# Two-layer decoder on one core: load and linear attention in one stage, recurrent weights fetched a stage earlier, four score banks in the second cross attention

## The reference

```python
x = x + linear_attention(layernorm(x))          # 16 heads of 8, causal, feature map elu + 1
x = x + cross_attention_0(layernorm(x), ctx)    # 16 heads of 8, one mask row per sequence
x = x + ternary_ffn(layernorm(x))               # gate and up 512, weights rounded to -1, 0, 1
x = x + mamba(layernorm(x))                     # 4 blocks, inner width 256, 16 states, scan over 256 tokens
x = x + cross_attention_1(ctx, layernorm(x))    # queries 16 heads of 64 from layernorm(x), keys and values from ctx
x = x + moe(layernorm(x))                       # top 2 of 8 experts
```

## Time and profile before

| what | us |
| --- | --- |
| median of 3 runs | 1855.62 |
| the profiled execution | 1858.3 |
| its span, from the first to the last instruction | 1856.6 |
| load stage, to the last VectorE instruction | 40.1 |
| linear attention, 40.3 to | 184.3 |
| cross attention 0, to | 415.6 |
| feed-forward and the norm after it, to | 503.3 |
| mamba, 503.6 to | 1430.7 |
| norm and cross attention 1, to | 1764.8 |
| experts and store, to | 1856.6 |

### The profile page before, as it was taken

How to read it: one execution, slowest core, us unless ns; L and a number is a source line. 1 busy time by engine, 2 the same in 40 slices (tenths; PEclk the granted TensorE clock), 3 DMA queues, 4 the chain that set the end, 5 groups by cost and what they waited for, 6 DMA issues and landing times. The chain is left out here.

```text
span 1856.6 us, 23408 instructions
## 1 busy us (share of the span) xinstructions
PE 1338.0 (72%) x6867; PEld 652.9 (35%) x6867; DVE 1443.7 (78%) x2462; ACT 1106.6 (60%) x2435; POOL 1141.6 (61%) x742
## 2 busy tenths in 40 slices
PE   3788898986655667766666765667655698899878
PEld 2555565653221222211222221222211365566523
DVE  3555588986419999999999999999997577777634
ACT  2444787875636666556666655666644577677630
POOL 2101466650039999999999999999995244444400
PEclk8889899996668778777788877888867899999979
DMA  3000000000044434354334434443431311111000
GB/s 96 1 1 2 1 2 2 1 2 1 21 168 179 153 116 172 140 206 183 125 141 163 177 154 183 180 146 117 168 130 57 130 46 47 64 73 46 1 0 23
DMA packets 68666, 168.04 MB, mean 91 GB/s; under 512 B 20404, under 2 KB 38088, under 8 KB 55112
## 3 DMA queue, kind: packets, MB, share of 16 engines
q1 hardware_dynamic: 65800, 164.34, 24.1%
q10 hardware_dynamic: 2496, 2.36, 0.4%
q0 software_dynamic: 256, 0.01, 0.0%
HBM read 131.03 MB, written 35.65 MB: 90 GB/s over the span
## 5 line engine op out<-in xcount | busy, mean ns | idle before, releaser
L1543 POOL TENSOR_TENSOR ma_hs<-ma_dtuR,ma_Bt 128x1024 f32<-128x1024 f32 x256 | 597.3, 2362 | 30.7 <-PE ps L1619 23.4
L1725 ACT ACTIVATE ps<-ma_dtR,ma_A 128x512 f32<-128x512 f32 x512 | 332.6, 682 | 314.5 <-DVE ma_hs L1867 271.1
L824 POOL TENSOR_TENSOR x_pr<-x_pr,x_rec 128x512 f32<-128x512 f32 x256 | 267.9, 1047 | 288.9 <-DVE x_rec L1064 288.9
L1861 DVE TENSOR_TENSOR_SCAN ps<-ps,ma_hs 128x1024 f32<-128x1024 f32 x176 | 401.8, 2283 | 2.0 <-POOL ma_hs L1543 1.9
L1030 ACT ACTIVATE x_pr<-x_sm,x_mx 128x256 f32<-128x256 f32 x512 | 255.2, 500 | 70.0 <-DVE x_mx L1055 67.3
L1619 PE MATMUL ps<-ma_hs,ma_fold 128*32 128x512 f32 x1024 | 164.4, 772 | 163.5 <-POOL ma_hs L1551 151.1
L1867 DVE TENSOR_TENSOR ma_hs<-ps,ma_Ct 128x1024 f32<-128x1024 f32 x176 | 215.4, 1224 | 6.1
L1586 PE MATMUL ps<-ma_hn,ma_w_tap 128*128 128x512 f32 (+3 forms) x256 | 146.3, 726 | 88.2 <-ACT ma_hn L1749 75.6
L1861 DVE TENSOR_TENSOR_SCAN ma_hs<-ps,ma_hs 128x1024 f32<-128x1024 f32 x80 | 182.5, 2281 | 30.9 <-ACT ps L1725 29.7
L1551 POOL TENSOR_TENSOR ma_hs<-ma_hs,ma_Ct 128x1024 f32<-128x1024 f32 x80 | 188.6, 2358 | 13.6 <-DVE ma_hs L1861 13.6
L886 PE MATMUL ps<-ident,x_pr 128*128 128x128 f32 x1024 | 162.1, 284 | 4.6 <-DVE x_pT L964 4.3
(11 more groups left out here) (303 smaller groups left out, 2231.0 us busy)
## 6 DMA issues: line engine op xcount, KB each, us to landing
ma_dtuR<-ma_dtu_d SPq DMA_DIRECT2D x32, 1024.0 KB, 6.7
ma_dtR<-ma_dt_d SPq DMA_DIRECT2D x32, 1024.0 KB, 8.8
ma_Bt<-ma_bc_d SPq DMA_DIRECT2D x16, 1024.0 KB, 5.1
ma_Ct<-ma_bc_d SPq DMA_DIRECT2D x16, 1024.0 KB, 7.4
ma_dtu_d<-ma_dtu SPq DMA_DIRECT2D x32, 256.0 KB, 2.0
ma_dt_d<-ma_dt SPq DMA_DIRECT2D x32, 256.0 KB, 2.3
keys_d<-ma_kv SPq DMA_DIRECT2D x32, 256.0 KB, 5.0
values_d<-ma_kv SPq DMA_DIRECT2D x32, 256.0 KB, 2.1
```

Of the source, the lines that this page charges most:

```text
L824: pool.tensor_tensor(pr[:, r, :, :], pr[:, r, :, :], rec[:, r, :].unsqueeze(2).broadcast_to([P, 2, L]), ALU.mult).then_inc(pr_done, 1)
L1543: pool.tensor_tensor(hs[:, k % SLOTS, :, :], dtuR[:, unit(f, h), q, :].unsqueeze(1).broadcast_to([P, 2, CH]), rows(Bt, k), ALU.mult).then_ ...
L1725: e = act.activation(c.ps[:, 2 * (k % 2) + a, :], dtR[:, unit(f, h), q, :], ACT.Exp, scale=A[:, (f // QUARTERS) % 2, h, q, no:no + 1])
L1861: dve.tensor_tensor_scan(out, pair(k), slot(k), 0.0, ALU.mult, ALU.add).then_inc(scan_done, 1)
```

## The change

Three edits. First, load and linear attention become one block, `opening_stage`. SP loads x in two halves, then the context, the mask row and the feed-forward weights. TensorE transposes x first; the context is transposed after the first projection. VectorE's work on the mask and the ternary weights is cut into pieces that `for_later(b, m)` puts behind the causal masking of given pairs; TensorE's part of it (`weight_mean`, `ternary_turned`) stands after the first pair of sequence 4 and before the last output projection. Scores j = 0 to 2 also wait for the copies that free their banks. Second, a class `RecurrentWeights` holds the mamba weights for the whole program; for block 0 its transfers are issued and its GpSimd work is done in the feed-forward stage, and `a_exp` is waited for in a part of its own (`rates`). Third, cross attention 1 takes the bank plan of cross attention 0: score pairs alternate between banks 0, 1 and 5, 7, values have bank 4 alone, projections and the output projection share bank 6, and the four projections stand one each at n = 9 to 12.

```diff
-def load_stage(c, g):
...
-def linear_attention_stage(c):
+def opening_stage(c, g):
...
+            @block.sync
+            def _(sp):
+                x = g["x"].rearrange("b (t p) d -> p (b t) d", p=P)
+                sp.dma_start(xt[:, 0:NT // 2, :], x[:, 0:NT // 2, :]).then_inc(x_in0, 16)
+                sp.dma_start(xt[:, NT // 2:NT, :], x[:, NT // 2:NT, :]).then_inc(x_in1, 16)
+                sp.dma_start(ct[:, :, :], g["ctx"].rearrange("b (t p) d -> p (b t) d", p=P)).then_inc(ctx_in, 16)
+                sp.dma_start(mi[:, :, :], g["m0"].rearrange("(a b) k -> a b k", a=1).broadcast_to([P, B, L])
+                             ).then_inc(mask_in, 16)
+                sp.dma_start(wg[:, 0:4, :], g["wg"].rearrange("(t p) d -> p t d", p=P)).then_inc(ffn_in, 16)
+                sp.dma_start(wg[:, 4:8, :], g["wu"].rearrange("(t p) d -> p t d", p=P)).then_inc(ffn_in, 16)
+                sp.dma_start(wd[:, :], g["wd"]).then_inc(ffn_in, 16)
...
+                for h in range(4):
+                    pe.wait_ge(x_in0 if h < 2 else x_in1, 16)
+                    for k in range(4):
+                        mm = pe.transpose(c.ps[:, 4 + h, k * P:(k + 1) * P], xt[:, 4 * h + k, :], c.ident[:, :])
+                    mm.then_inc(x_turned, 1)
+                for h in range(4):
+                    pe.wait_ge((x_dve, x_act)[h % 2], 1 + h // 2)
+                    pe.matmul(c.ps[:, 4 + h, :], c.centre[:, :], c.xT[:, chunk(h)], start=True, stop=True).then_inc(centred, 1)
+                pe.wait_ge(wa_in, 16 * 9)
+                for n in range(2):
+                    for k in range(4):
+                        mm = pe.transpose(c.ps[:, 2 + n, k * P:(k + 1) * P], wa[:, 4 * n + k, :], c.ident[:, :])
+                    mm.then_inc(wa_turned, 1)
+                for h in range(2):
+                    pe.wait_ge(squared, h + 1)
+                    pe.matmul(c.ps[:, h, :], c.average[:, :], sq[:, chunk(h)], start=True, stop=True).then_inc(var_done, 1)
+                pe.wait_ge(wa_copied, 4)
+                pe.wait_ge(squared, 3)
...
+                def context_turned():
+                    pe.wait_ge(ctx_in, 16)
+                    for n in range(4):
+                        for k in range(4):
+                            mm = pe.transpose(c.ps[:, 2 + n, k * P:(k + 1) * P], ct[:, 4 * n + k, :], c.ident[:, :])
+                        mm.then_inc(ctx_turned, 1)
+
+                def weight_mean():
+                    pe.wait_ge(sums, 3)
+                    pe.wait_ge(v_done, 5)
+                    pe.wait_ge(rec_done, 5)
+                    pe.wait_ge(x_done, 3)
+                    pe.matmul(c.ps[:, W, 0:3], c.ones_sq[:, :], part[:, :], start=True, stop=True).then_inc(mean_done, 1)
...
+                def ternary_turned():
+                    pe.wait_ge(ternary, 3)
+                    pe.wait_ge(sc_act, B * NPAIR - 1)
+                    pe.wait_ge(sc_dve, B * NPAIR - 1)
...
                 pe.wait_ge(made, 10)
                 project(0)
+                context_turned()
                 project_values(0)
                 denominator(0)
                 for b in range(B):
                     for m in range(NPAIR):
                         score(b, m)
+                        if b == 4 and m == 0:
+                            weight_mean()
...
                 weigh(B - 1, NG - 1)
+                ternary_turned()
                 out_projection(B - 1)
 
             @block.scalar
             def _(act):
+                for i, n in enumerate(("aq", "ak", "av", "ao", "xq", "xk", "xv", "xo")):
+                    act.dma_start(wa[:, i, :], g[n]).then_inc(wa_in, 16)
+                act.dma_start(wr[:, :], g["rw"]).then_inc(wa_in, 16)
+                act.preload_act_table_set("natural_log_exp_and_others")
...
+                def for_later(b, m):
+                    if (b, m) == (0, 6):
+                        dve.wait_ge(mask_in, 16)
+                        dve.tensor_scalar(c.maskrow[:, :, :], mi[:, :, :], 0.0, MASKED, ALU.is_equal, ALU.mult).then_inc(mask_done, 1)
+                    if (b, m) == (1, 6):
+                        dve.wait_ge(mask_done, 1)
+                        dve.tensor_reduce(c.present[:, :], c.maskrow[:, :, :], AX.X, ALU.max).then_inc(mask_done, 1)
+                    if (b, m) == (2, 0):
...
+                    if (b, m) == (4, 0):
+                        dve.wait_ge(mean_done, 1)
+                        dve.tensor_scalar(c.wmean[:, :], c.ps[:, W, 0:3], 1.0 / (F * P), 1e-5, ALU.mult, ALU.max).then_inc(step, 1)
+                    if (b, m) == (4, 3):
+                        dve.wait_ge(step, 1)
+                        dve.reciprocal(wscale[:, :], c.wmean[:, :]).then_inc(step, 1)
...
+                    if (b, m) == (5, 6):
+                        dve.wait_ge(step, 5)
+                        dve.tensor_scalar(wq[:, :, F:2 * F], wq[:, :, 0:F], ROUND, 1.0, ALU.subtract, ALU.min).then_inc(step, 1)
...
+                        for_later(b, m)
                 divide(B - 1)
+                dve.wait_ge(qturned, 1)
+                dve.tensor_copy(c.wguT[:, :], c.psb(2)[:, 0:8 * P]).then_inc(qcopied, 1)
+                dve.tensor_copy(c.wdT[:, :, :], c.psb(4)[:, 0:4 * P].rearrange("p (t d) -> p t d", t=4)).then_inc(qcopied, 1)
...
-    WO = 6 if small else 7
-    SCORE_BANKS = ((0, 1), (5, 7)) if small else ((0, 1),)
+    WO = 6
+    SCORE_BANKS = ((0, 1), (5, 7))
...
-            a = n - FIRST_UNIT
-            if small:
-                return range(a - 1, a) if 1 <= a <= NP else range(0)
-            return range(min(NP, a * 3 // 2), min(NP, (a + 1) * 3 // 2)) if a >= 0 else range(0)
+            a = n - FIRST_UNIT - 1
...
-            return SCORE_BANKS[(n // 2) % len(SCORE_BANKS)][n % 2]
-
-        def projection_bank(n):
-
-            return 6 if small else 6 + n % 2
+            return SCORE_BANKS[(n // 2) % 2][n % 2]
...
-                    bank = c.ps[:, projection_bank(n), :]
-                    if small and n >= 1:
+                    bank = c.ps[:, WO, :]
+                    if n >= 1 or not first:
                         pe.wait_ge(evac, b * NP + n)
-                    elif n >= 2:
-                        pe.wait_ge(evac, b * NP + n - 1)
-                    elif not first:
-                        pe.wait_ge(evac, b * NP)
-                    if 6 + n == WO and not first and not second:
+                    if n == 0 and not first and not second:
...
-                    if small and (n >= 4 or not first):
-                        pe.wait_ge(max_done, b * NH + n - 2)
-                    elif not small and (n >= 2 or not first):
-                        pe.wait_ge(s_free, b * NH + n)
+                    if n >= 4 or not first:
+                        pe.wait_ge(max_done if small else s_free, b * NH + n - 2)
...
-                    if not small and g % 2 == 0 and (g >= 4 or not first):
-                        pe.wait_ge(oT_done, b * NO + g // 2 - 1)
+                    if not small and g % 2 == 0 and (g >= 2 or not first):
+                        pe.wait_ge(oT_done, b * NO + g // 2)
...
-                                mm = pe.matmul(c.ps[64 * r:64 * r + 64, O0 + h // 4 % 2, at:at + L],
+                                mm = pe.matmul(c.ps[64 * r:64 * r + 64, O0, at:at + L],
...
-                                        c.ps[:, O0 + u % 2, :]).then_inc(oT_done, 1)
+                                        c.ps[:, O0, :]).then_inc(oT_done, 1)
...
+            @block.sync
+            def _(sp):
+                c.weights.load(sp, g, 0)
+
+            @block.gpsimd
+            def _(pool):
+                c.weights.prepare(pool, c, 0)
...
+    def load(self, sp, g, i):
+        b, xb, gq, e32 = i % 2, RANK + 2 * NS, 4, 32
+        done = self.weights_in
+        if i >= 1:
+            sp.wait_ge(self.tap_w, 3 * i)
+            sp.wait_ge(done, self.LOADS * i)
+        sp.dma_start(self.w_in[:, :], g["m_in"][i]).then_inc(done, 16)
+        sp.dma_start(self.cwb[:, :, :], g["m_cw"][i].rearrange("(a c) t -> a c t", a=1).broadcast_to([P, DI, TAPS])).then_inc(done, 16)
...
+    def prepare(self, pool, c, i):
+        b, gq = i % 2, 4
+        pool.wait_ge(self.weights_in, self.LOADS * (i + 1))
+        for h in range(2):
...
-                load(0)
                 kv_weight(sp, 0)
...
-                weights(0)
+                rates(0)
```

397 lines of the change are left out of this document (176 added, 221 removed).

## The result

| | us |
| --- | --- |
| median before, same chip | 1854.9 |
| median after | 1829.99 (1829.32 to 1834.84) |
| ratio after to before | 0.9859, interval 0.984 to 0.9877 |
| the profiled execution after, span | 1829.81, 1828.1 |

A forecast was written before the change was run, and what follows sets the result against it. Small waits set linear attention, with TensorE nearest its limit; VectorE limits mamba. Opening -20.9, recurrent weights -9.5, GpSimd +0.3 and cross attention 1 -3.7 sum to -33.8, from 1855.6 to 1821.8 us, range 1811 to 1834.

The forecast's parts named there:

- First projection: Start of linear attention: with x sent first, the first projection starts at 21.9 in place of 44.84, -22.9 us.
- centre product about 1.05 to its square: Opening's norm: after ScalarE's copy the centre product takes about 1.05 us to its square, reaching 14.0; first average at 15.0.
- Pieces in linear attention: About 10 us of VectorE's mask and ternary weight work moved into linear attention costs +2.0 us, bounds 0 and +10.
- The first rival: Opening's extra VectorE work falls on TensorE's waits, its clock drops, x lands later: +10 us, 1831.8; chance 0.18.
- Recurrent weights: Start of mamba: block 0's weights are ready early, so TensorE begins at 510.6 in place of 520.16, -9.5 us.
- GpSimd beside VectorE: Feed-forward stage: GpSimd's weight work delays a few VectorE SBUF-to-SBUF instructions, +0.3 us, bounds 0 and +2.9.
- Cross attention 1: New plan of score, value and projection banks in cross attention 1: -3.7 us together, bounds -15 and +38.
- Before the first scores: Cross attention 1's first sequence: four projections through one bank take 7.1 us in place of 4.5, +2.4 us.
- The wait of 1.63 goes: Cross attention 1: VectorE's 1.63 us wait at n = 10 goes, since one projection more stood before it.
- The scores of n = 12 come 1.0 - 0.1 earlier: Cross attention 1: one of four projections falls behind the scores of n = 12; over a whole sequence -0.5 us.
- The second rival: Score banks free cross attention 1, TensorE's sum sets it: 2.1 us for each of seven sequences, 1810.6; chance 0.09.
- The third: Cross attention 1: one value bank makes TensorE late at 32 copy waits, +38 us in place of -3.7, 1864; chance 0.04.

The follow-up runs named there:

- e3: Kernel before with only cross attention 1's new plan of banks and projections: 1858.6 us against 1857.27, ratio 1.0008.
- e8: Changed kernel with each long piece of VectorE's mask and weight work in linear attention run twice: 1832.62 us, ratio 0.9870.
- e2: Changed kernel with cross attention 1 back in its old plan of banks and projections: 1830.49 us, ratio 0.9834.
- e5: Changed kernel with GpSimd's weights made at mamba's start and cross attention 1's first four projections in banks 6, 7, 5, 4 without waits: 1823.54 us, ratio 0.9807.
- e6: As e5, with cross attention 1's output projection in four parts and query projections at n = 9, 11, 13, 14: 1814.87 us, ratio 0.9762.
- e10: Changed kernel with GpSimd's weights made at mamba's start and cross attention 1 in its old plan: 1827.97 us, ratio 0.9836.
- e11: As e10, with the output projection in four parts and query projections at n = 9, 11, 13, 14, on the old banks: 1811.5 us, ratio 0.9748.
- e12: As e5, with cross attention 1's four query projections one step later, at n = 10 to 13: 1821.1 us, ratio 0.9803.
- e7: Changed kernel with GpSimd's 2.85 us instruction in the feed-forward stage run twice in a row: ratio 0.9869.
- e1: Opening alone against the kernel before, recurrent weights back in mamba and cross attention 1 in its old plan: 1833.8 us against 1857.27, ratio 0.9859.
- e4: Changed kernel with weight transfers kept in the feed-forward stage but GpSimd's part made at mamba's start: 1833.33 us, ratio 0.9858.
- e9: Changed kernel repeated word for word: 1833.98 us against 1856.64, ratio 0.9872.

## Why the prediction was right or wrong, step by step

The time lay in the range (1811 to 1834), 8 us over the forecast, and faster as forecast. The two gains that made the time, the opening and the recurrent weights, came by their mechanism. But the sum hid errors that ran against each other: cross attention 1 was 11 us off its term, and 4.8 us of the experts and most of what linear attention gave came from the clock, which no term had. That these nearly met was luck. No run separates the parts of the opening (x sent first, the boundary gone, the weights later); they are shown together.

**First projection, right in mechanism, 2.0 short.** -20.9 where -22.9 stood. The second half of x was copied out at 12.38, 0.6 earlier than forecast. What failed is the step "centre product about 1.05 to its square": the four products of `centre` were taken as one to wait for, and all eight instructions, 4.80 us, and the attention weights stand ahead of the average (17.05 in place of 15.0).

**Pieces in linear attention, about half the cost, and hidden by the clock.** Forecast +2.0, measured -2.4 in the two profiles. The stretches of one sequence tell the two causes apart. Before, six low stretches of the clock, one in each later sequence, make it 17.06 us; e3, with the same code, ran at 16.55 at a clock of 1.00. After, the sequences at 1.00 take 16.55 as well, but for two: the one behind the reduction, 17.10 where e3 has 16.44, and the one with `weight_mean`, 17.02 where e3 has 16.56. So the pieces cost about 1.1 us there; the first two sequences can't be compared, since the clock was low in them at different times. The stretch with the reduction was +0.7 where I had +1.1, the one with `weight_mean` +0.5 where I had nothing (0.32 of it is TensorE's own work for it), and the last copies show nothing where I had +0.4: the last stretch, from the last `xn,wqk` on, is 29.05 us in the seven traces without a low stretch of the clock in it, and 29.56 to 29.71 in the seven with one, before and e3 (no pieces) among them. The first rival, +10 for the opening, is refuted at this amount; e8 shows where it begins to bite. Its clause on the clock did not come true: the granted clock of the stage was higher in after than in before (0.98 against 0.89). Since e2, with the same code in this stage as after, had 0.94 and 140.05 us, and e3, with the code of before, 0.95 and 137.60, the clock is not shown to be a gain of the change, only of an execution.

**Recurrent weights, right.** -8.6 against -9.5; in the six traces (e5, e6, e8, e10, e11, e12) where the first norm's `centre` product took 1.10 us, as in before, and not 2.05, the start of mamba took 7.15, which is -9.4. What was late next was `hn`, as said.

**GpSimd beside VectorE, wrong.** I took +0.3 from the earlier trace rows and kept the price by the Trainium skill, up to 2.86, apart. It was 1.8 us: the first tensor-with-scalar instruction of VectorE from SBUF to SBUF was shut out to the end of GpSimd's, and e7 did it a second time for 2.6 us. I should have looked for which VectorE instruction starts inside which GpSimd one. The Trainium skill, page "SBUF — State Buffer", section "SBUF: two separate sides", says that the pair is taken for a whole instruction and the other engine fully blocks, and that of VectorE's instructions only some need it. The rows agree with the first for two instructions: 1.92 and 2.73 us, each to the end of GpSimd's 2.85. They agree with the second too: of VectorE's two reductions out of PSUM from 406.29 on, 1.31 us together, the later one lay inside GpSimd's instruction, and one took 0.69 before. But not every pair was held to the end: beside GpSimd's next two instructions (`ma_dD`, 409.50 to 410.93) `ffn_s_gate` and the scaling behind it took 0.26 and 0.33 us, where they took 0.14 and 0.23 before. No run here tells why. The row I had used showed only the end of a GpSimd instruction, 0.34 us of it, and a loss of 0.20.

**Cross attention 1, the gain wasn't there.** -3.7 forecast, +7.6 in the two traces, -1.7 to +4.5 by the time of e3. The sum itself was 0.4 too good: six times -0.5 is -3.0, where it has -3.2, and 7.1 less 4.5 is 2.6, where it has +2.4. Its parts:
- Before the first scores I had +2.4 and it was +6.5. The serial chain through one bank was forecast; the high clock in it was not to be had. At the like clock (7.2 to 7.4 in seven traces) the chain costs 3.7. e5 takes it away. Behind them VectorE's waits in the first sequence fell from 3.5 to 0.9 us, where I had 3.0 less.
- "The wait of 1.63 goes": it fell to 0.67 only. By the order in front of the prediction two projections less stand before the scores of n = 10 (one where there were three), and not one, as the prediction counts; even so 0.67 us of the wait stayed. The first projection now has the output projection's bank and waits 0.74 us for VectorE's residual addition. I had listed the new waits on the value bank and left this one out. e12 moves the projection off it and gains 0.8 a sequence.
- "The scores of n = 12 come 1.0 - 0.1 earlier": counted from those of n = 8 they came 10.04 us later where it was 10.10, so 0.06 earlier. The same 0.74 stands ahead of them. VectorE, which gained 1.0 us at n = 10, lost 0.9 of it again at n = 12 (1.50 for 0.58). At n = 14, where I gave 0.2 back, it doesn't wait. So a middle sequence took 36.3 to 36.8 us and not 35.7; the old plan has 36.2 to 36.5.

The second rival (the banks free the stage) is refuted by the period, and e11 against e6 says more: given an even order, the old banks are the faster in the trace (33.7 against 34.7). The third (one bank for values makes it slower) was right in its mechanism, but 0.24 us a sequence (the wait at n = 8, 2.89 for 2.65), far from its price of 38.

**The experts were in no term.** 4.8 us of the 28.5 between the two spans come from code that isn't changed. Nine traces have 84.2 to 84.7 there, four 79.6 to 80.5 and e12 83.1. By the runs after is 24 to 26 us faster than before. The ledger of causes: opening -23 (e1), start of mamba -9, GpSimd's hold +1.8 in the trace (e4, e7), the new plan about +4 (e10 against e9, less the hold): -26. The last entry isn't shown clear of noise: the intervals of e9 and e10 touch, e3 has +1.5, and from the first projection of cross attention 1 to the experts the traces with the new plan have 309 to 316 us, those with the old one 307 to 314.

What stays open: why e4's 1.8 us don't show in its time, and what of the new plan's cost is real beyond the first scores, since e3 allows -1.7 to +4.5 us.

## What to carry to other kernels

Buffers for one producer come out of another's: before giving a stream more banks, list every wait that the banks taken away will make, the shared bank's last reader too, and ask if TensorE isn't rather held by the order of its work. Here an even order was worth 9 us (e6 against e5) and 16 us (e11 against e10), and more score banks nothing. When work moves to GpSimd beside VectorE, look for each small tensor-with-scalar instruction of VectorE from SBUF to SBUF in that stretch: here two of them, of 0.17 and 0.14 us, lasted to the end of a GpSimd instruction of 2.85 us. And take no price of a few us on TensorE from one execution whose clock you haven't read.

## What the runs showed of the hardware that was not expected

TensorE's clock falls in different places in executions of the same code: linear attention, word for word the same in e2 and after, ran at 0.94 and at 0.98, and took 140.05 and 137.29 us. In the kernel before it fell once in one sequence after another, for about 3 us, as here (the first row's clock is 0.53, the 13.6 us ahead of it have 0.99):

```profile
112.60:116.00 3.40, 3.40 (x30) 2.07 (x28) 2.36 (x2) 1.18 (x3) 0.00 (x0) 0.53 0.02 5
99.00:112.60 13.60, 10.96 (x116) 7.63 (x114) 6.67 (x11) 6.51 (x16) 1.58 (x2) 0.99 0.01 1
```

In cross attention 1 one period of seven is 3.5 to 6 us longer than the rest in thirteen of the fourteen traces, with the old plan and the new (40.96 before, 41.14 after). It is the one in which the loop over sequence pairs jumps back. VectorE's first instruction behind the jump stands idle before it, 2.3 to 2.8 us in these thirteen, and for nothing that the profile shows:

```profile
1584.56 0.43 DVE L1117 TENSOR_SCALAR x_neg<-x_m 128x512 f32 x1 [2.51 <-issue]
```

e8 is the exception: all its periods between middle sequences are 36.3 to 36.8, its instruction there has no such wait, and its stage is 4.5 us shorter than in after. Why, no run here tells.
